# Transposing transfers issued by ScalarE, seven groups in the ternary stage, earlier chains of the fourth pair, gates behind slot 7

## What is computed

```python
xn = (x - mean(x)) / sqrt(var(x) + eps)          # over D = 2048; x is [8, 4096, 2048]
a = tanh(xn @ Wa.T + ba); b = tanh(xn @ Wb.T + bb)   # S = 64 each
h[t] = a[t] * h[t-1] + b[t]                      # scan over 4096 tokens
attn = xn + h @ Wout.T + bout
scale = mean(abs(weight))                        # weight is [2048, 2048]
w_t = clip(round(weight / (scale + 1e-10)), -1, 1)
ffn = xn @ (w_t * scale).T + bias
return x + attn + ffn
```

## Time and profile before

| | us |
|---|---|
| runs | 550.02, 546.73, 548.99; median 548.99 |
| profiled execution | 545.46 |
| its span, slowest core (3), from which the rows are | 543.9 |
| spans of cores 0 to 7 | 535.8, 539.3, 539.8, 543.9, 541.5, 536.1, 539.9, 543.6 |

### The profile page before, as it was taken

One profiled execution on the slowest core, in us unless ns is written; L12 is line 12 of the kernel. 1 busy time (PEld: TensorE's weight loads), 2 busy tenths in 40 slices (PEclk: granted clock), 3 DMA queues, 4 the chain that ended last, 5 costly groups with the idle time before them and its releaser, 6 DMA issues.

```text
span 543.9 us, 8281 instructions; the slowest of 8 cores (535.8 to 543.9 us)
## 1 busy us (share of the span) xinstructions
PE 467.0 (86%) x2323; PEld 223.9 (41%) x2323; DVE 341.8 (63%) x516; ACT 215.8 (40%) x183; POOL 150.3 (28%) x536
## 2 busy tenths in 40 slices
PE   0020489999939999999999999999999999999997
PEld 0010134545424444444444545454545444545443
DVE  2633497969737574857576767666666757573633
ACT  0477395745434334252506070706161615242000
POOL 0400236331634051414233232323241415150000
PEclk9999999999979999999999999999999999999999
DMA  7999980264464948585777667676858584843212
GB/s 225 341 331 344 303 217 1 78 218 112 117 144 152 209 156 219 149 221 156 221 158 213 174 183 205 189 199 174 215 164 224 160 228 155 232 145 88 107 49 116
DMA packets 72048, 99.15 MB, mean 182 GB/s; under 512 B 57090, under 2 KB 57090, under 8 KB 65986
## 3 DMA queue, kind: packets, MB, share of 16 engines
q1 hardware_dynamic: 71328, 97.53, 61.3%
q0 software_dynamic: 384, 1.05, 1.2%
q10 hardware_dynamic: 292, 0.05, 0.1%
HBM read 52.48 MB, written 33.55 MB: 158 GB/s over the span
## 4 chain that ended last, share of the span: by engine, by line
PE 57%; DMA 15%; SPq 10%; issue 4%; POOLq 4%; DVE 4%; ACT 3%; DVEq 2%; POOL 0%; ACTq 0%
PE pu L714 44%; DMA wbuf<-wt 6%; DMA xnT<-wbuf 5%; PE pu L686 5%; PE pab L673 4%; SPq L265 4%; SPq L257 3%; DMA y<-sx 3%; DVE bst L439 2%; ACT wbuf L337 2%; DMA sx<-x 1%; SPq L270 1%; DVEq L441 1%; PE pu L732 1%; PE pu L727 1%
## 5 line engine op out<-in xcount | busy, mean ns | idle before, releaser
L455 DVE SCALAR_TENSOR_TENSOR sx<-pu,scl,sx 128x512 f32<-128x512 f32 x212 | 158.0, 748 | 147.1 <-PE pu L714 80.0
L714 PE MATMUL pu<-wbuf 128*128 128x512 f16 x896 | 204.7, 379 | 0.0
L714 PE MATMUL pu<-wbuf,xnT 128*128 128x512 f16 x672 | 154.2, 379 | 0.0
L714 PEld LDWEIGHTS pu<-wbuf 128*128 128x128 f16 x896 | 87.5, 98 | 103.3
L714 PEld LDWEIGHTS pu<-wbuf,xnT 128*128 128x128 f16 x672 | 65.6, 98 | 79.6
L439 DVE BATCH_NORM_STATS2 bst<-sx 128x6 f32<-128x512 f32 x128 | 78.8, 678 | 14.4 <-DMA sx<-x 14.2
L337 ACT ACTIVATE wbuf<-sx,nmr,yr 128x2048 f16<-128x2048 f32 x26 | 54.3, 2088 | 37.6 <-DMA xnT<-wbuf 31.2
L840 POOL TENSOR_SCALAR uu<-mv 128x1 f32<-128x1 f32 (+1 forms) x29 | 10.1, 348 | 209.5 <-DVE mv L443 201.1
L344 ACT ACTIVATE sx<-sx,nmr,p1r 128x2048 f32<-128x2048 f32 x32 | 66.9, 2093 | 2.4
L686 PE MATMUL pu<-wbuf,xnT 128*128 128x512 f16 x256 | 57.9, 379 | 3.7 <-DVE wbuf L490 2.0
L356 ACT ACTIVATE sa<-pab,bab_s 64x256 f32<-64x256 f32 x16 | 7.5, 468 | 117.8 <-PE pab L673 117.8
(11 more groups left out here) (62 smaller groups left out, 309.6 us busy)
## 6 DMA issues: line engine op xcount, KB each, us to landing
sx<-x SPq DMA_DIRECT2D x32, 1024.0 KB, 6.5
y<-sx SPq DMA_DIRECT2D x63, 512.0 KB, 3.7
wbuf<-wt SPq DMA_DIRECT2D x15, 1024.0 KB, 30.3
wbuf<-wt SPq DMA_DIRECT2D x2, 512.0 KB, 33.5
xnT<-wbuf SPq DMA_TRANSPOSE x52, 3.5
wab_s<-wab POOLq DMA_DIRECT2D x1, 512.0 KB, 12.7
y<-sx SPq DMA_DIRECT2D x2, 256.0 KB, 2.5
wocv<-wo POOLq DMA_DIRECT2D x1, 256.0 KB, 14.6
```

What stands on the lines that cost most here:

```text
L455: vector.scalar_tensor_tensor(out, bank(b), scl[:, :], out, OP.mult, OP.add).then_inc(s_ev, 1)
L714: ins = tensor.matmul(bank(b), left(p, lname, c), right(rname, c, h), start=(fresh and c == 0), stop=(state is None and c == HC - 1), skip ...
```

## The change

Five things are altered.

- **The transfers.** `turn(t)` with its two DMAs moves from SP's program to ScalarE's. There it stands behind norm(a) in pair n, and for b + 2 behind norm(b + 2) (turn(7): behind states(2)). SP keeps loads and stores. norm(7) moves from behind states(2) to between evict_T(5, 1) and resid(5).
- **The ternary stage.** TensorE keeps seven groups open instead of six (`NFIRST`). The seventh is unit (1, 2), first in `PLAIN`, in the bank that the transposes use (`pt`, bank 6 in `PBANK`). turn(2, 0) on TensorE waits for its eviction. The plain units and transposes of tiles 2 and 3 stand closer together. VectorE rounds five slices, ScalarE eleven. The first half of slice 0 is clamped as soon as its own rounding is done. stats(2) and stats(3) come at slices 5 and 8, and stats(4), stats(5) ahead of the first evictions. The stats of tiles 7 and 6 and two sums move by some places.
- **The chains.** chain(2, 3) becomes chain(2) and chain(3), and norm(2), norm(3) wait for their own. chain(7) and chain(6) come ahead of the transfers of `wo2`.
- **The gates.** gate(n) stands behind slot 7 instead of 6.
- **The scan.** scan(n) stands behind take(p, 9) instead of take(p, 8).

```diff
--- before.py
+++ after.py
...
 N_AA = len(ABS_ACT) + 2
 N_AD = len(ABS_DVE) + 2
-RND_DVE = [0, 3, 6, 9, 12, 15]
+RND_DVE = [0, 4, 8, 12, 15]
 RND_ACT = [c for c in range(NCH) if c not in RND_DVE]
-PLAIN = [(t, q) for t in range(3) for q in range(NQ)] + [(3, 2), (3, 3), (3, 0), (3, 1)]
+PLAIN = ([(1, 2)] + [(0, q) for q in range(NQ)] + [(1, 0), (1, 1), (1, 3)]
+         + [(2, q) for q in range(NQ)] + [(3, 2), (3, 3), (3, 0), (3, 1)])
 NPL = len(PLAIN)
+NFIRST = 7
+PBANK = [6] + [i % NBANK for i in range(NPL - 1)]
...
         two_i = sb("two_i", [128, 2], I32)
         shi = sb("shi", [128, 2], I32)
         pu = e(nc.psum_tensor("pu", [128, NBANK * QW], F32))
-        ptr = e(nc.psum_tensor("ptr", [128, 1024], F16))
+        pt = e(nc.psum_tensor("pt", [128, QW], F32))
         pab = e(nc.psum_tensor("pab", [128, 512], F32))
         s_x = [sem(f"s_x{i}") for i in range(NSX)]
...
         s_v = sem("s_v")
         block = e(nc.Block())
+        ptr = pt[:, :].bitcast(F16)
         def wslot(c):
             return wbuf[:, c * D:(c + 1) * D]
...
             return xnT[:, (t % 4) * D + lo:(t % 4) * D + hi]
         def bank(b):
+            if b == NBANK:
+                return pt[:, :]
             return pu[:, b * QW:(b + 1) * QW]
         def sfac(n, i):
...
                 sync.wait_ge(s_ev, evicted)
                 sync.dma_start(out=y_d[TT * t:TT * (t + 1), lo:hi], in_=xs(t, lo, hi)
                                ).then_inc(s_st[t % NSX], 16)
-            def turn(t):
-                sync.wait_ge(s_xnb, POS[t] + 1)
-                sync.wait_ge(s_unit, last_use(t - 4))
-                for half in range(2):
-                    sync.dma_start_transpose(
-                        out=xT(t, half * HD, (half + 1) * HD).rearrange(
-                            "p (c w) -> p c w", c=HC),
-                        in_=xnb[:, half, :]).then_inc(s_dt, 16)
             load(0)
             load(1)
...
                 if t == 1:
                     load(7)
                     load(6)
-            turn(7)
             for p in range(2, NP):
-                n, m = p + 1, p + 2
+                m = p + 2
                 a, b = 2 * p, 2 * p + 1
                 if m < NP:
                     load(2 * m + 1)
-                if n < NP:
-                    turn(2 * n)
-                if m < NP:
                     load(2 * m)
                 store(a, 0, HD, unit_no(p, 3))
                 store(b, HD, D, unit_no(p, 9))
-                if m < NP:
-                    turn(2 * m + 1)
                 store(b, 0, HD, unit_no(p, 11))
                 if p + 1 < NP:
                     store(a, HD, D, unit_no(p, 13))
...
             scalar.dma_start(out=xs(5)[64:65, :], in_=bi_d[:, :]).then_inc(s_bi, 16)
             def norm(t):
-                scalar.wait_ge(s_stats, POS[t] + 1 if t >= TURNED else t // 2 * 2 + 2)
+                scalar.wait_ge(s_stats, POS[t] + 1 if t >= TURNED or t in (2, 3) else
+                               t // 2 * 2 + 2)
                 if t == 3:
                     scalar.wait_ge(s_tern, NCH + 1)
...
                 scalar.activation(xs(t), xs(t), AF.Identity, bias=nmr[:, i:i + 1],
                                   scale=p1r[:, i:i + 1]).then_inc(s_v, 1)
+            def turn(t):
+                scalar.wait_ge(s_xnb, POS[t] + 1)
+                scalar.wait_ge(s_unit, last_use(t - 4))
+                for half in range(2):
+                    scalar.dma_start_transpose(
+                        out=xT(t, half * HD, (half + 1) * HD).rearrange(
+                            "p (c w) -> p c w", c=HC),
+                        in_=xnb[:, half, :]).then_inc(s_dt, 16)
             def evict_T(t, half):
                 scalar.wait_ge(s_tr, 2 * POS[t] + half + 1)
-                scalar.copy(xT(t, half * HD, (half + 1) * HD), ptr[:, :]
+                scalar.copy(xT(t, half * HD, (half + 1) * HD), ptr
                             ).then_inc(s_xnT, 1)
             def gates(n):
...
                     resid(a)
                     evict_T(b, 0)
                     evict_T(b, 1)
+                    if n == 2:
+                        norm(7)
                     resid(b)
                 else:
                     norm(a)
+                    turn(a)
                     resid(a)
                 gates(n)
                 states(n)
-                if TURNED // 2 <= n + 1 < NP:
+                if 4 <= n + 1 < NP:
                     norm(b + 2)
+                if 3 <= n + 1 < NP:
+                    turn(b + 2)
                     resid(b + 2)
         @block.vector
...
                 t, q = PLAIN[u]
                 vector.wait_ge(s_v, POS[t] + 1)
                 vector.wait_ge(s_unit, u + 1)
-                add_to(xs(t, q * QW, (q + 1) * QW), u % NBANK)
+                add_to(xs(t, q * QW, (q + 1) * QW), PBANK[u])
             def take(p, k):
                 t, lo = target(p, k)
...
             vector.drain()
             vector.reciprocal(inv[:, :], scl[:, :]).then_inc(s_inv, 1)
             vector.drain()
-            for lo in (0, HD):
+            for i, lo in enumerate((0, HD)):
                 vector.tensor_scalar(wint[:, lo:lo + HD], wslot(0)[:, lo:lo + HD],
                                      inv[:, :], None, OP.mult).then_inc(s_rnv, 1)
-            for i, lo in enumerate((0, HD)):
-                vector.wait_ge(s_rnv, 2)
+                vector.wait_ge(s_rnv, i + 1)
                 vector.tensor_scalar(wpart(0, lo, lo + HD), wint[:, lo:lo + HD],
                                      -1.0, 1.0, OP.max, OP.min).then_inc(s_tern, 1)
             for c in range(NCH):
                 if c > 0:
                     ternary(c)
-                if c == 3:
+                if c == 5:
                     stats(2)
-                elif c == 6:
+                elif c == 8:
                     stats(3)
                 elif c == 13:
                     scan(0)
...
                 if c + 2 in RND_DVE:
                     rounded(c + 2)
-            for u in range(6):
-                plain(u)
             stats(4)
             stats(5)
+            for u in range(NFIRST):
+                plain(u)
+            plain(7)
             for c in range(0, HC, 2):
                 t1(c)
-            plain(6)
-            plain(7)
             scan(1)
             t3(0)
             t3(2)
             plain(8)
             plain(9)
+            stats(ORD[6])
             t3(4)
             t3(6)
             plain(10)
+            stats(ORD[7])
             plain(11)
-            stats(ORD[6])
-            stats(ORD[7])
             vector.wait_ge(s_T, 8)
             t2(0)
+            t2(2)
             plain(12)
-            t2(2)
             plain(13)
             t2(4)
...
                 if m < NP:
                     stats(2 * m)
                 take(p, 8)
+                take(p, 9)
                 if n < NP:
                     scan(n)
-                take(p, 9)
-                if n < NP:
                     s13(n)
                 take(p, 10)
                 if n < NP:
...
                     tensor.wait_ge(s_xnb, POS[t] + 1)
                 if POS[t] > 0 or half > 0:
                     tensor.wait_ge(s_xnT, 2 * POS[t] + half)
+                if t == 2 and half == 0:
+                    tensor.wait_ge(s_ev, 1)
                 for c in range(8):
                     lo = half * HD + 128 * c
                     ins = tensor.transpose(ptr[:, 128 * c:128 * (c + 1)],
...
             def plain_part(u, lo, hi):
                 t, q = PLAIN[u]
-                b = u % NBANK
+                b = PBANK[u]
                 if lo == 0:
                     if b in used:
                         tensor.wait_ge(s_ev, used[b])
...
             def plain_mix(u):
                 t, q = PLAIN[u]
                 tensor.wait_ge(s_hsb, t // 2 + 1)
-                tensor.matmul(bank(u % NBANK), hA[:, (t % 4) * TT:(t % 4 + 1) * TT],
+                tensor.matmul(bank(PBANK[u]), hA[:, (t % 4) * TT:(t % 4 + 1) * TT],
                               wocv[:, q * QW:(q + 1) * QW], start=False, stop=True
                               ).then_inc(s_unit, 1)
...
             for c in range(NCH):
                 if c == 0:
                     tensor.wait_ge(s_tern, 1)
-                    for u in (0, 1, 4, 5):
+                    for u in (1, 2, 5, 6):
                         plain_part(u, 0, 1)
                     tensor.wait_ge(s_tern, 2)
-                    for u in (2, 3):
+                    for u in (3, 4, 0):
                         plain_part(u, 0, 1)
                 else:
                     tensor.wait_ge(s_tern, c + 2)
-                    for u in range(6):
+                    for u in range(NFIRST):
                         plain_part(u, c, c + 1)
                 if c == 6:
                     tensor.wait_ge(s_wabl, 16)
...
             tensor.wait_ge(s_brow, 1)
             tensor.wait_ge(s_hrow, 1)
             tensor.wait_ge(s_wol, 16)
```

(19 more changed lines are left out.)

## The result

| | runs | median us | ratio to the kernel before, 95% interval |
|---|---|---|---|
| before | 4 | 548.03 | |
| changed | 4 | 638.49 (636.31 to 642.86) | 1.166 (1.158 to 1.173) |

The changed kernel is slower by 90 us; the prediction was 537, with 545 as the upper end. The loss is on all eight cores, with spans of 615.1 to 641.3.

The account below looks back on a forecast made before the run. TensorE was taken as busiest, its own work the floor at 27.67 us between gates, with waits for transposing transfers on top. -0.3 - 7.3 - 4.2 = -11.8 gave 532.1 on the profiled core; forecast 537, range 532 to 545.

Parts of the forecast that it names:

- Ternary stage: Seven groups: first matmul at 67.7, stage end at 96.6, 1.7 us won of 3.7, then 2.1 us of new waits.
- What the ternary part is worth: Net effect of the ternary stage up to the loop's start: -0.3 us, bounds -1.7 and +1.3.
- gate(3): Fourth pair's gate matmuls: wait and slow run of 9.6 us become 2.3 at full clock, -7.3; bounds 0, and 5.8 plus 1.3.
- the landing L: Time for a transposing transfer to land in the loop: 3.5 us taken, longest seen 8.5.
- the 7.19: Landing time in us of turn(a)'s second half behind a 1 MB load on SP, in the kernel before.
- The circle of dependences: Loop chain from gate to gate, 15.3 + 2L: 22.3 us at L = 3.5, fits into 27.67 until L = 6.2.
- Rival (c): Transposes in their own queue starve beside loads or stores; 15.3 + 2L bounds the loop, 561 at L = 7.2; chance 0.08.
- -4.2 from the new queue: Later pairs' gates: all later waits for transposing transfers go once ScalarE issues them, -4.2 us; other bound 0.
- The rule that I weighed: Transfers of all issuers share 16 engines, only issue time is saved; if strict, the 4.2 us stay, sum about 541.

## Why the prediction was wrong

- **Ternary stage.** It held. I put the first matmul at 67.7, its end at 96.6 and the new waits at 2.1 us. The changed kernel, timeline of TensorE, answering to the earlier trace rows:

```profile
67.48 1.02 PE L696 MATMUL pu<-wbuf,xnT 128*128 128x512 f16 x4 [0.98 <-DVE wbuf L570]
...
96.71 0.61 PE L669 MATMUL pt<-sidn,xnT 128*128 128x128 f16 x8 [0.19 <-DVE sx L466]
...
104.36 0.61 PE L669 MATMUL pt<-sidn,xnT 128*128 128x128 f16 x8 [0.53 <-ACT xnT L354]
...
137.74 5.34 PE L724 MATMUL pu<-wbuf,xnT 128*128 128x512 f16 x24
```

  The waits were 0.7 us and the loop began at 137.74, 1.2 sooner than forecast. I had taken two things too long: chain(3) ran for 6 us on POOL where I had 10, and VectorE began the first eviction at 95.8 where I had 96.4.
- **What the ternary part is worth.** Wrong by its reach. I costed it up to the loop's start alone, at -0.3, and put the earlier loads and stats under the chains. With the transposes on SP it is worth 9 to 10 us. On the slowest core more than half of that has come together by gate(3), most of it because the transfers of the fourth pair are late without it; the rest comes in later pairs and is not explained.
- **gate(3).** The forecast of 2.3 us at full clock, from a start at 155.5, is close to what the kernel with the transposes on SP does (1.3 to 2.7 and mostly at full clock in one run, 1.0 to 4.1 and mostly not in the other). The changed kernel waited 8.14 and took 3.26, beyond my bound of 5.8 and 1.3. The order of events up to the issue was right: norm(6) at 148.12 where I had 147.0, turn(6) from 150.34 where I had 149.2. The transfer was not.
- **The step that failed** is the landing L. I took its worst case from the longest landing in the trace, 8.5, and its likely one from half a share of 2.7 us of engine time. The first is of a transfer that stood behind a load in one queue, the second of transposes with nothing beside them. The prediction says itself that no row has transposes beside a load of another queue, and yet it used 8.5 as the bound. Measured there: up to 19.1, and engine time for the same packets up by 64% (76 to 125 us). The sum's other figure for a busy neighbour, the 7.19, counts from the start of the second half's issue, not from its end as I wrote; it is from one queue too. What bounds an operation from rows where its neighbours are queued does not bound it where they are beside it.
- **The circle of dependences** was the right frame. 15.3 + 2L is full at L = 6.2. With 3.8 for tile b and 18.2 for tile a it gives 37.3, and gate(4) and gate(5), between which these two fall, start 40.2 apart, 1.2 of it for the slow gate(4) (3.11 for 1.91). Rival (c) was this mechanism with its threshold, and it was priced at 561 for L = 7.2. It got 0.08, as I judged that tile b's transfers meet no load. Tile a's alone are enough. It should have had the chance of an unmeasured quantity whose threshold (6.2) lies under a value already seen (8.5).
- **-4.2 from the new queue** came out as +76 us of waits. What does remove later waits is the gates' place behind slot 7 with the later scan, some 4 to 5 us in all with the transposes on SP, which my sum put down to the new queue.
- **The rule that I weighed.** The Trainium skill (DMA: Bandwidth & Descriptors, section Issuing engines are not separate DMA queues) says that a further issuer saves issue time only. No run shows a gain from the second queue, which agrees. But the loss is outside that rule as well: by it I had 541.

What stays open is why a load issued behind transposes of another queue stretches both, with the engines mostly idle at the end. The stores and the issuing engine are ruled out as the cause by runs. So is the role of the queues as a condition of it, though not as a part of its size (604 against 550), and so is the row size of the loads as what sets the landings. The inside of an engine was not seen.

## What to carry to other kernels

Keep transposing transfers and large loads in one queue, in an order you choose. A second queue is no relief where the two kinds overlap, and before moving one, check for each transfer what will be issued into the other queue while it is in flight. If the trace has no row for an operation beside its new neighbour, its landing has no upper bound from that trace: measure it in one run of that edit alone before the rest is judged, and compute at what landing time the loop of dependences is full. Parts bundled with a bad one can be good: without the transfers' move this change gives 2%, 535.9 and 537.3 against 546.3 and 549.0.

## What the runs showed of the hardware

- 52 transposing transfers of 256 KB took 76 to 77 us of the 16 engines with small loads or none beside them (1.5 us each), and 125 with loads issued beside them from the other queue. Landings went from 3.2 to 7 us to as much as 19, and 22.7 in the run with one load held back.
- The same load behind the same transposes did little harm in one queue (landings up to 9.6 with both on ScalarE, 11.2 in the worst run with both on SP) and cost about 90 us in two.
- After pauses of TensorE of under 2 us the next gate took 1.91 in nearly all cases. After 2.0 to 4.6 it took anything from 1.91 to 3.57, and after more than 5 us 3.1 to 3.6 (all cores of all runs).
